# Three cross-attention loops that also normalise their finished tiles

## What is computed

```
h = x + MultiHead16x16(layernorm(x), ctx)          # L0x and L3x with Wq, Wk, Wv, Wo; L2x without
layernorm(x) = (x - mean) / sqrt(var + 1e-5)        # over the 256 columns of a row

L0:  n = layernorm(h);  h = h + n;  y = LinearAttention(layernorm(n) * gamma + beta)
L2:  y = HeadAttention(layernorm(h))                # RMS-normalised heads, softmax
L3:  y = GatedRecurrence(layernorm(h))
```

## Time and profile before

| | us |
|---|---|
| median of three runs | 2843.96 |
| lowest and highest | 2843.69, 2849.13 |
| span of the profiled execution | 2855.1 |
| PE busy | 2474.5 (87%) |
| DVE busy | 1714.1 (60%) |
| ACT busy | 1399.2 (49%) |
| POOL busy | 663.0 (23%) |

### The profile page before, as it was taken

The page is one execution under the profiler, slowest core; times in us unless marked ns, Lnnn a source line. Parts: engine busy times, 40 slices in busy tenths (PEclk is TensorE's granted clock), DMA queues, the critical chain, the costliest instruction groups (busy, mean ns, idle before and its releaser), DMA issues. The chain is left out here.

```text
span 2855.1 us, 83215 instructions
## 1 busy us (share of the span) xinstructions
PE 2474.5 (87%) x35827; PEld 2086.5 (73%) x35827; DVE 1714.1 (60%) x3397; ACT 1399.2 (49%) x3496; POOL 663.0 (23%) x862
## 2 busy tenths in 40 slices
PE   6999787999967999999997748987996776999888
PEld 4888555777746899988996648975775645999567
DVE  6777675566656333333324755657885776777663
ACT  3887324455532444444432324425884453777342
POOL 3111002212102300000000202432336535555200
PEclk9999899999988999999998859997999898999999
DMA  2110003112021100000000042333321001111100
GB/s 79 36 36 21 17 0 96 52 42 62 3 62 59 45 17 17 17 17 17 2 2 24 3 143 75 122 108 104 93 73 52 2 2 47 53 52 48 45 1 30
DMA packets 118221, 126.66 MB, mean 44 GB/s; under 512 B 10877, under 2 KB 110152, under 8 KB 117864
## 3 DMA queue, kind: packets, MB, share of 16 engines
q1 hardware_dynamic: 114024, 110.93, 12.5%
q0 software_dynamic: 3840, 10.49, 1.2%
HBM read 105.67 MB, written 15.73 MB: 43 GB/s over the span
## 5 line engine op out<-in xcount | busy, mean ns | idle before, releaser
L1030 ACT ACTIVATE s_ca_probs<-s_ca_scores,s_ca_neg_max 128x256 f32<-128x256 f32 x768 | 353.4, 478 | 34.2 <-DVE s_ca_neg_max L1074 23.9
L1074 DVE TENSOR_REDUCE s_ca_neg_max<-s_ca_scores 128x4 f32<-128x1024 f32 x192 | 234.2, 1221 | 52.6 <-PE s_ca_scores L936 25.7
L953 PE MATMUL s_ca_probs_flipped<-identity,s_ca_probs 128*128 128x128 f32 x1536 | 214.1, 283 | 11.5 <-ACT s_ca_probs L1030 10.5
L2063 DVE COPY s_mx_w_mixed<-s_mx_ps 128x512 f32<-128x512 f32 x256 | 163.6, 684 | 95.6 <-PE s_mx_ps L1910 80.9
L953 PEld LDWEIGHTS s_ca_probs_flipped<-identity,s_ca_probs 128*128 128x128 f32 x1536 | 168.1, 143 | 49.9 <-ACT s_ca_probs L1030 22.9
L2018 ACT COPY s_mx_w_mixed<-s_mx_ps 128x512 f32<-128x512 f32 x256 | 137.3, 589 | 118.9 <-PE s_mx_ps L1897 97.6
L1030 ACT ACTIVATION_READ_ACCUMULATOR s_ca_probs<-s_ca_scores,s_ca_neg_max 128x1 f32 x768 | 160.0, 208 | 0.0
L620 PE MATMUL s_ln_flip<-identity,s_ln_xn 128*128 128x128 f32 x352 | 63.0, 357 | 108.2 <-DVE s_ln_xn L602 107.7
L1037 ACT COPY s_ca_probsT<-s_ca_probs_flipped 128x512 f32<-128x512 f32 x192 | 115.2, 600 | 79.3 <-PE s_ca_probs_flipped L953 79.3
L857 POOL TENSOR_TENSOR s_ca_inv_spread<-s_ca_inv_sums,h_ca_own_half 128x128 f32<-128x128 f32 x192 | 72.7, 400 | 342.6 <-DVE s_ca_inv_sums L1096 342.6
L82 PE MATMUL s_cc_shared<-s_cc_ctxT_low,h_cc_wkv_high 128*128 128x256 f32 x512 | 145.9, 285 | 2.2 <-DVE s_cc_ctxT_low L1425 2.2
(11 more groups left out here) (513 smaller groups left out, 7378.5 us busy)
## 6 DMA issues: line engine op xcount, KB each, us to landing
h_ca_ctxT<-in_ctxT SPq DMA_DIRECT2D x96, 256.0 KB, 3.3
h_mx_w_by_input<-in_L_ffn_eW1T SPq DMA_DIRECT2D x16, 512.0 KB, 5.4
h_mx_w_by_hidden<-in_L_ffn_eW2T SPq DMA_DIRECT2D x8, 1024.0 KB
h_re_win<-in_L_ffn_W_in SPq DMA_DIRECT2D x8, 1024.0 KB
h_ca_ctx<-in_ctx SPq DMA_DIRECT2D x32, 256.0 KB, 2.7
x_normed_transposed<-in_ctx SPq DMA_DIRECT2D x7, 1024.0 KB, 5.5
h_re_wout<-in_L_ffn_W_out SPq DMA_DIRECT2D x8, 512.0 KB
choice_results<-s_rt_zeros SPq DMA_DIRECT2D x4, 1024.0 KB, 10.5
```

Source lines behind the costliest of these rows:

```text
L953: last = nc.tensor.transpose(psT[u % len(psT)][:, 2 * a + c, :], PR[b % 2][:, 4 * n + 2 * h + a, c * P:(c + 1) * P], ident[:, :])
L1030: last = nc.scalar.activation(PR[b % 2][:, p, :], psS[:, p // 2, (p % 2) * NKEY:(p % 2 + 1) * NKEY], ACT.Exp, bias=nmax[b % 2][:, p:p + 1] ...
L1074: nc.vector.tensor_reduce(nmax[b % 2][:, 4 * n:4 * n + 4], psS[:, 2 * n:2 * n + 2, :].rearrange("p r (g k) -> p r g k", g=GR), AX_X, ALU.m ...
L2063: last = nc.vector.tensor_copy(part(int(name[1]), r), bank(j, r))
```

## The change

A new class `TileNorm` holds the normalisation of one tile at a time. In the three cross-attention loops DVE's `statistics` also forms mean and variance, half the variance and a first guess of the inverse root from its bits. POOL improves it in three Newton steps and scales the tile, in each odd pass from the fourth, between `spread_inverse(b)` and `spread(b+2)`. PE flips the tile two passes later, right behind `flip(b, 0)`, and ACT stores it. Tile 14 follows behind the last pass, and tile 15 within the next stage: on POOL at the start of `linear_attention` and `gated_recurrence`, and behind `low(2)` in `normed_heads`. The three `layernorm_transposed` stages are left out. Their loads are issued at the start of the loop before, on SP, ahead of the loop's own loads; `HeadWeights.prepare` runs in two halves in the first two passes of L2x. The semaphores of a weight object are now given back when it ends, together with those of stages.

The diff, cut to its core:

```diff
+class TileNorm:
+    MAGIC = 0x5f3759df - 0x400000
+    STEPS = 3
...
+    def load(self, sp):
+        if self.affine:
+            for n, v in enumerate(self.affine):
+                sp.dma_start(self.col[:, n, :], v).then_inc(self.s_col, 16)
+
+    def statistics(self, dve, i):
+        n = self.roots
+        half, bits, root = self.half[:, i, :], self.bits[:, i, :], self.root[:, i, :]
+        link = Chain(dve, self.s_dve, i * (n + 2))
+        dve.bn_stats(self.ST[:, i, :], self.X[:, i, :]).then_inc(self.s_st, 1)
+        dve.wait_ge(self.s_st, i + 1)
+        link(dve.bn_aggr(self.MV[:, i, :], self.ST[:, i, :]))
+        link(dve.tensor_scalar(half[:, 0:1], self.MV[:, i, 1:2], 0.5, 0.5 * EPS, ALU.mult, ALU.add))
+        if n == 2:
+            link(dve.tensor_scalar(half[:, 1:2], self.MV[:, i, 1:2], 0.5 * (1.0 + EPS), 0.5 * EPS * EPS, ALU.mult, ALU.add))
+        link(dve.tensor_scalar(bits, half.bitcast(I32), 1, None, ALU.logical_shift_right))
+        dve.tensor_scalar(root.bitcast(I32), bits, -1.0, float(self.MAGIC), ALU.mult, ALU.add).then_inc(self.s_root, 1)
+
+    def normalise(self, pool, i):
+        half, root, step = self.half[:, i, :], self.root[:, i, :], self.step[:, i, :]
...
+        link = Chain(pool, self.s_pool, i * (4 * self.STEPS + 1 + 2 * self.residual))
+        pool.wait_ge(self.s_root, i + 1)
+        for _ in range(self.STEPS):
+            link(pool.tensor_tensor(step, root, root, ALU.mult))
+            link(pool.tensor_tensor(step, step, half, ALU.mult))
+            link(pool.tensor_scalar(step, step, -1.0, 1.5, ALU.mult, ALU.add))
+            link(pool.tensor_tensor(root, root, step, ALU.mult))
+        if self.residual:
+            link(pool.tensor_scalar(gain, root[:, 0:1], 1.0, 1.0, ALU.mult, ALU.add))
+            link(pool.tensor_scalar(back, mean, root[:, 0:1], -1.0, ALU.mult, ALU.mult))
+        link(pool.tensor_scalar(shift, mean, root[:, last:last + 1], -1.0, ALU.mult, ALU.mult))
+        if i >= 2:
+            pool.wait_ge(self.s_f, i - 1)
+        pool.tensor_scalar(self.XN[i % 2][:, :], x, root[:, last:last + 1], shift, ALU.mult, ALU.add).then_inc(self.s_n, 1)
+        if self.residual:
+            pool.wait_ge(self.s_n, i + 1)
+            pool.tensor_scalar(x, x, gain, back, ALU.mult, ALU.add).then_inc(self.s_back, 1)
+
+    def flip(self, pe, i, dst):
+        pe.wait_ge(self.s_n, i + 1)
+        for c in range(KC):
+            last = pe.transpose(dst[:, c, :], self.XN[i % 2][:, c * P:(c + 1) * P], self.ident[:, :])
+        last.then_inc(self.s_f, 1)
+
+    def store(self, act, i, src):
+        act.wait_ge(self.s_f, i + 1)
...
+        last.then_inc(self.s_out, 1)

 def cross_attention(...)            # SP
+                for weights in loads:
+                    weights.load(sp)
+                norm.load(sp)
                 for b in range(NB):
                     load(b)
                                     # POOL
                 for b in range(NB):
                     spread_inverse(b)
+                    if ahead and b < KC:
+                        ahead(pool, b)
+                    if b >= 3 and b % 2:
+                        norm.normalise(pool, (b - 3) // 2)
                     if b + 2 < NB:
                         spread(b + 2)
                                     # PE
                     flip(b, 0)
+                    if b >= 5 and b % 2:
+                        pe.wait_ge(s_at, b)
+                        pe.wait_ge(s_we, (b - 1) // 2)
+                        norm.flip(pe, (b - 5) // 2, psN)
...
+                    if b >= 5 and b % 2:
+                        pe.wait_ge(norm.s_out, (b - 5) // 2 + 1)
                     attend(b)
+                norm.flip(pe, TILES - 2, psNT)
                 finish(TILES - 1)
                                     # ACT
                     turned(b, 0)
+                    if b >= 5 and b % 2:
+                        norm.store(act, (b - 5) // 2, psN)
...
+                norm.store(act, TILES - 2, psNT)
                                     # DVE
                 def statistics(i):
                     dve.wait_ge(s_we, i + 1)
-                    nc.vector.bn_stats(ST[:, i, :], X[:, i, :])
+                    norm.statistics(dve, i)

 def normed_heads(...)               # POOL
                 low(2)
+                norm.normalise(pool, LAST)

 def gated_recurrence(...)           # POOL
+                norm.normalise(pool, TILES - 1)
                 aside.prepare(pool)

 def perceiver(...)                  # L3, as one of the three
-                    layernorm_transposed(nc, X, XNT, ident, ST, loads=(w, f))
+                        cross_attention(nc, X, ST, QT, ident, ones, w, norm, mask=mask4, loads=(a, f))
```

More of the change, by code:

```diff
@@ L410, in load, with prepare @@
         sp.dma_start(self.WQK[:, :], d["L2_attn_wqk_col"]).then_inc(self.s_w, 16)
-    def prepare(self, pool):
+    def prepare(self, pool, c):
         pool.wait_ge(self.s_wq, 16)
[L414 to L417, removed]
+        pool.tensor_copy(self.WH[:, c, :], self.W[:, c, :]).then_inc(self.s_wh, 1)
+        pool.wait_ge(self.s_wh, c + 1)
+        pool.tensor_tensor(self.WL[:, c, :], self.W[:, c, :], self.WH[:, c, :].bitcast(F32), ALU.subtract).then_inc(self.s_wl, 1)
 class SoftmaxWeights:
@@ L754, in _, with cross_attention @@
                         low_input(t + 2)
-def cross_attention(nc, X, ST, QT, ident, ones, held, mask=None):
+def cross_attention(nc, X, ST, QT, ident, ones, held, norm, mask=None, loads=(), ahead=None):
     OWN = held.OWN
@@ L1489, in _, with linear_attention @@
                 row_statistics(TILES - 1)
-def linear_attention(nc, X, ST, XNT, ident, held):
+def linear_attention(nc, X, ST, XNT, ident, held, norm):
     LAST = TILES - 1
@@ L1588, in _ @@
                 attend(0)
+                norm.flip(pe, LAST, psN)
                 body(1, 0)
@@ L3286, in _, with gated_recurrence @@
                     nc.vector.tensor_tensor(x, psX[u % 2][:, :, :], x, ALU.add).then_inc(s_x, 1)
-def gated_recurrence(nc, X, ST, XNT, ident, held, aside):
+def gated_recurrence(nc, X, ST, XNT, ident, held, aside, norm):
     TC = 512
@@ L3605, in perceiver @@
         mask4 = d["mask_Bx1x1xS2_fk0"].rearrange("(t b) c e s -> t b (c e s)", b=2)
-        if "L0x" in STAGES:
+        with held(nc, kept) as (sb, sem):
+            a = LinearWeights(sb, sem, d)
+            norm = TileNorm(sb, sem, X, XNT, ident, ST, twice=True, residual=True, affine=(d["L0_attn_gamma_col"], d["L0_attn_beta_col"]))
             with held(nc, kept) as (sb, sem):
@@ L3613, in perceiver @@
                     project_transposed(nc, XNT, QT, q, KC, aside=w)
[L3614 to L3620, removed]
+                    cross_attention(nc, X, ST, QT, ident, ones, w, norm, loads=(a,))
+            linear_attention(nc, X, ST, XNT, ident, a, norm)
         if "L0f" in STAGES:
@@ L3653, in perceiver @@
                 routed_experts(nc, X, ST, XNT, XN, ident, w)
-        if "L2x" in STAGES:
+        with held(nc, kept) as (sb, sem):
+            t = TileWeights(sb, sem, d)
             with held(nc, kept) as (sb, sem):
[L3656 to L3659, removed]
-            with held(nc, kept) as (sb, sem):
[L3661 to L3668, removed]
-                            softmax_attention(nc, X, ST, QKT, VA, ident, w)
-                if "L2f" in STAGES:
-                    layernorm_transposed(nc, X, XNT, ident, ST, by_position=True, loads=() if "L2a" in STAGES else (t,))
-                    tiled_experts(nc, X, XNT, ident, WHICH, BT, t)
@@ new lines, in perceiver @@
+                norm = TileNorm(sb, sem, X, XNT, ident, ST)
+                with held(nc, kept) as (sb, sem):
+                    w = CrossWeights(sb, sem, d, ctx4, ctx=ctxn)
+                    layernorm_transposed(nc, X, XNT, ident, ST, loads=(w,), prepare=w.prepare)
+                    cross_attention(nc, X, ST, XNT, ident, ones, w, norm, loads=(h, a, t), ahead=h.prepare)
+                with nc.sbuf_tensor("l2a_qkT", [P, 4, TOKENS], F32) as QKT, \
+                        nc.sbuf_tensor("l2a_v", [P, TILES, 8, 4, 16], F32) as VA:
+                    normed_heads(nc, X, XNT, QKT, VA, ident, h, a, norm)
+                    softmax_attention(nc, X, ST, QKT, VA, ident, a)
```

77 lines of the change are left out of this document (59 added, 18 removed).

## The result

The changed kernel takes 2983.34 us (median; 2979.81 to 2984.43), beside 2846.55 us of the kernel before in the same runs: a ratio of 1.0466, 95% interval 1.0449 to 1.0483. Forecast were 2922 us with a range of 2845 to 2985. The direction was right, the time lies 1.7 us inside the range, and the loss was 137 us where 78 were worked out.

A forecast was written before the change was run, and what follows sets the result against it. PE bounds the kernel, busy 87% of 2855.1 us, chained with POOL in the loops. Pairs 91.6, ends 10.2, mask 9, last tile 4 and 2, less 38.3 for removed stages: +78.5, scaled to 2922 us; range 2845 to 2985.

The forecast's parts named there:

- The place and the waits: PE's scores wait for POOL in every other pass of L0x, L2x, L3x: 1.41, 1.93, 3.21 us, 14 times each.
- The tiny step: One tiny chained POOL instruction of normalise: 0.28 us taken, low end 0.19, high end 0.49.
- The cheap: Rival: a tiny POOL instruction takes 0.11 to 0.24 us; 0.19 gives 2870 us; chance 0.22.
- the hidden rivals: Rival: POOL overlaps chained instructions, 0.06 us each, so the loop hides the work; 2833 us, faster; chance 0.13.
- DVE's chain: Statistics on DVE delay POOL's odd pass: 0.85 us more, 1.06 in L0x; wrong if POOL starts no later.
- What it does to each pair of passes: Added POOL and DVE time less slack, 14 pairs per loop: 19.7, 27.0, 44.9 us in L0x, L2x, L3x; sum 91.6.
- the dear rival: Tiny POOL instruction above 0.33 us, POOL waiting for DVE, or PE's clock falling: 2985 to about 3055 us; chance 0.17.
- ACT and PE: In the loops, ACT's store has cover and PE's flips are hidden in the wait already priced; otherwise flips cost 0.45 us.
- The low case: Pair cost at the low tiny instruction of 0.19 us: PE's own transposes and hand-over 0.45 us in L0x; loops sum 45.5.
- The end of L0x: PE's flip of tile 14 waits for POOL's normalise(14), delaying finish(15): +3.5 us; three loops 10.2.
- L3x's start: First mask of L3x queued on SP behind seven weight transfers: +9 us (8 to 9.9; 0 if not held back).
- the 16 us allowed for: DVE's L1089 blocked by wide POOL instructions in L0x and L3x, 0.56 us once per pair: at most 16 us, 2938.

The follow-up runs named there:

- behind: Changed kernel with normalise of an odd pass moved on POOL behind spread(b+2) and the mask rows: 2853.99 us, ratio 1.0014 to the kernel before.
- warm: Changed kernel with idle PE transposes in the waits for POOL, 12 in L2x and 24 in L3x per even pass: 2937.34 us, ratio 1.0306.
- mask_first: Changed kernel with the first two masks of L3x issued on SP ahead of the next stages' weights: 2974.27 us, ratio 1.0440.

## Why the prediction was right, and where its sum was short

**The place and the waits: right.** The forecast of 14 waits of 1.41, 1.93 and 3.21 us is answered by 20.4 / 14 = 1.46 us in L0x, (20.8 - 2.4) / 14 = 1.3 in L2x (most are 1.42) and (51.5 - 7.3) / 14 = 3.16 in L3x, the longest wait being the loop's start in the last two. In L2x PE waits less than forecast; with the clock up, in warm, an even and an odd pass still take 13.2 us together, 1.8 more than before; 0.3 of that is PE's own flip. **behind** shows that these waits and what hangs on them are 129 of the 137 us.

**The tiny step: right.** It was taken as 0.28 us from a line through two wide instructions; the groups of the changed kernel give 0.19 us and the timeline a pitch of 0.27:

```profile
L588 POOL TENSOR_TENSOR h_tn_newton_step<-h_tn_inverse_root 128x1 f32<-128x1 f32 x96 | 18.5, 193 | 9.5 <-SPq L3420 4.5
...
L588 POOL TENSOR_TENSOR h_tn_newton_step<-h_tn_inverse_root 128x2 f32<-128x2 f32 x48 | 9.3, 194 | 2.5
...
L595 POOL TENSOR_SCALAR h_tn_shift<-h_tn_mean_variance,h_tn_inverse_root 128x1 f32<-128x1 f32 x48 | 12.5, 261 | 5.0
```

The Trainium skill's page "GPSIMD Engine Reference", 3.1 Elementwise — side-by-side cycle accounting, leads to some 60 ns fixed, an estimate from its figures, and so to 0.15 us a step; this trace gives 193 ns for one element, and the measurement decides. The cheap and the hidden rivals went with it.

**DVE's chain: right.** The forecast would have been wrong if POOL's odd pass started no later than before. From DVE's addition to x to POOL's next spread_inverse it is (median) 6.87, 4.73 and 6.66 us in L0x, L2x and L3x, where 5.87, 4.08 and 5.87 stood: 1.00, 0.65 and 0.79 us later, against 1.06, 0.85 and 0.85 worked out. The chain itself in L3x: start of bn_stats to start of the next instruction, once 0.34 us, is 2573.43 - 2572.31 = 1.12, so 0.78 us more, where 0.85 was worked out:

```profile
2572.31 0.42 DVE L572 BATCH_NORM_STATS2 x_statistics<-x_resident 128x6 f32<-128x256 f32 x1
...
2573.36 0.15 DVE L579 TENSOR_SCALAR h_tn_inverse_root<-h_tn_half_bits 128x1 int32<-128x1 int32 x1
2573.43 0.68 DVE L1179 COPY s_ca_probsT<-s_ca_probs_flipped 128x512 f32<-128x512 f32 x1
```

**What a wait costs: the term that was short.** "What it does to each pair of passes" priced a wait at its own length. DVE's attended results of passes 1 and 31 of L3x, before and after:

```profile
2427.74 0.29 DVE L1104 TENSOR_TENSOR s_ca_attendedT<-s_ca_out,s_ca_inv_sumsT 128x128 f32<-128x128 f32 x1
...
2661.11 0.29 DVE L1104 TENSOR_TENSOR s_ca_attendedT<-s_ca_out,s_ca_inv_sumsT 128x128 f32<-128x128 f32 x1
```

```profile
2477.08 0.29 DVE L1203 TENSOR_TENSOR s_ca_attendedT<-s_ca_out,s_ca_inv_sumsT 128x128 f32<-128x128 f32 x1
...
2786.91 0.29 DVE L1203 TENSOR_TENSOR s_ca_attendedT<-s_ca_out,s_ca_inv_sumsT 128x128 f32<-128x128 f32 x1
```

That is 233.4 us before and 309.8 after. From pass 1 to pass 31 the loops grew by 25.8, 41.5 and 76.5 us, 1.8, 3.0 and 5.5 for each of 14 pairs, not by 1.41, 1.93 and 3.21: 144 us in place of 92. The prediction had the clock falling in PE's new gaps as one of three reasons for the dear rival, and left it out of the forecast's sum; rows of the three short stages at 0.64 to 0.74 were there to give it a price. warm puts the term at 46 us; there, with the clock up, the loops grew by 25.8, 25.0 and 49.9 us between the same two results, 101 us together, so without the clock the pairs cost 9 us more than the 92 worked out.

The sum with that term is 78.5 + 46 = 125, and the two profiled spans differ by 125.9. That they agree so closely is luck. The windows from PE's last instruction of linear_attention to its first of L2x, before and after, hold stages that the change leaves alone:

```profile
426.76:1951.13 1524.37, 1326.20 (x20574) 1153.61 (x20575) 771.87 (x1539) 622.11 (x1136) 244.45 (x237) 0.93 0.16 48
```

```profile
441.59:1956.56 1514.97, 1321.91 (x20576) 1152.49 (x20575) 771.75 (x1539) 621.95 (x1136) 247.74 (x237) 0.93 0.16 49
```

The execution profiled before was 9.4 us longer there. Without that the spans differ by 135 us, near the 137 of the medians, and the other 12 us lie in the odd passes, where the prediction took PE's flips as hidden, and in the smaller terms.

It is luck, too, that 2983 us lies within the range: its top, 2985, was worked out for a tiny step of 0.38 us, but the step came to 0.27 and the rest of the time was the clock's.

**PE's flips: not hidden.** "ACT and PE" had them hidden in the wait. But PE waits in the even pass and flips in the odd one, and in the changed kernel the odd passes take 7.53, 5.85 and 7.76 us, where 7.24, 5.57 and 7.47 stood: 0.3 us a pair, 12 us over the three loops. In L2x and L3x it is the flip: pass 3, which has none yet, takes 5.57 and 7.47 us as before. In L0x pass 3 takes 7.50 us already, and what lengthens it there was not settled. The low case had 0.45.

**The smaller terms.** The end of L0x: PE's flip waits 3.17 us for POOL's last rows, 3.5 forecast; in L2x and L3x it is 2.7 and 2.5. L3x's start: 9.1 us by mask_first, 9 forecast. normed_heads: 69.05 us against 63.4 before, 5.6 for 4; gated_recurrence: 60.9 against 56.4, 4.4 for 2. Not in the sum were the change-overs at which all engines stand idle for 1 to 2.5 us, loads apart. They are seven in place of six, 11.6 us together in place of 9.3; behind L2x it is 1.82 us, where 1.71 stood before behind the normalisation. That clearing semaphores makes them long is likely, but was not measured by itself. linear_attention became 1.6 us shorter, for which nothing was forecast.

**Contention: small.** DVE's one recurring instruction with two SBUF inputs in these loops, before and after:

```profile
L1089 DVE TENSOR_TENSOR h_ca_ctxT_low<-h_ca_ctxT,h_ca_ctxT_high 128x512 fp32r<-128x512 f32 x60 | 41.7, 695 | 48.6 <-ACT h_ca_ctxT_high L1049 48.6
```

```profile
L1188 DVE TENSOR_TENSOR h_ca_ctxT_low<-h_ca_ctxT,h_ca_ctxT_high 128x512 fp32r<-128x512 f32 x60 | 44.9, 748 | 49.0 <-ACT h_ca_ctxT_high L1145 49.0
```

It took 53 ns longer, 3.2 us over 60 of them, far below the 16 us allowed for. In the changed kernel the 32 that ran with no POOL instruction beside them took 680 to 694 ns; the 28 that ran beside one took 811 on the mean, 24 of them 727 to 918. The Trainium skill's page "SBUF — State Buffer", Who interferes with whom, has such instructions contend with GpSimd's reads; the trace agrees.

## What to carry to other kernels

An engine that is busy 23% has room on average and none in front of the instruction that the bound engine waits for: before work is put on it, read how long before its need each of its results is ready, and put the new work behind the one with the least slack. When a chain makes TensorE wait in every turn of a loop, price the wait and, separately, the work behind it at the lower clock; idle matmuls in the gap are a cheap way to see which part is the clock. A load that is moved ahead in a queue is paid for by the first small load behind it.

## What the runs showed of the hardware

In L3x waits of 3.16 us brought PE's granted clock from 1.00 to 0.50 for the matmuls behind them, and the mean of the loop to 0.89; waits of 1.46 us in L0x left it at 0.99, while waits of 1.46 us and less in L2x went with 0.88: the clock fell behind 6 of the 14, and these even passes took 9.7 to 10.7 us, the other 8 took 6.7 to 7.4. With two steps, in the same loop, one wait of 2.09 us was followed by the half and one of 2.11 us by the full clock. So the length of the wait alone does not tell, and what else does was not settled here. Filling the waits with idle matmuls held the clock at 0.97. On POOL a tensor_tensor on one element for each partition took 193 ns and on two 194. If tiles shared their Newton steps, two might so be had for the time of one; this was not tried.
